# An adaLN block with a test-time-training layer and a mixture of experts: where the updated expert weights live, and how many expert blocks are worked beside the last chunk

## The reference, cut to what matters

```python
h = _layernorm(x) * (1 + ca) + sa
x = x + ga * attn(h)      # 2 sequences of 1024 rows, 4 heads of 128
h = _layernorm(x) * (1 + cb) + sb
x = x + gb * ffn(h)       # 8 experts, the best 2 for each row

# attn: a scan over chunks of 128 rows; state w0, w1, w2 for each head
def step(carry, inp):
    gate = ki @ w0_ ; hb = ki @ w2_ ; hidden = silu(gate) * hb
    dhidden = vi @ w1_.T   # and the gradients from it
    w1g = newtonschulz5(hidden*lr1 , vi) ; w0g = ... ; w2g = ...   # 2 steps, bf16
    w_i = (w_i + w_ig), each column scaled back to its first norm
    oi = silu(qi @ w0_) * (qi @ w2_) @ w1_

# ffn: each expert's weights carry a low-rank addition
gup = xf @ gate_up_proj[e] + 2 * (xf @ A_e.T) @ B_e.T
out = (silu(gates) * up) @ down_proj[e] + 2 * (...)
y   = out[best] * w0 + out[second] * w1       # the two best of softmax(router)
```

## Time and profile before

| | |
|---|---|
| time, three runs | 967.18, 969.18, 971.17 us |
| the profiled execution | 967.96 us |
| its span, first to last instruction | 966.2 us |
| TensorE busy | 863.2 us, 89% |
| VectorE, ScalarE, GpSimdE busy | 68%, 67%, 36% |
| moved by DMA | 120.41 MB |

### The profile page before, as it was taken

How to read it: one execution, slowest core, us unless ns; L and a number is a source line. 1 busy time by engine, 2 the same in 40 slices (tenths; PEclk the granted TensorE clock), 3 DMA queues, 4 the chain that set the end, 5 groups by cost and what they waited for, 6 DMA issues and landing times.

```text
span 966.2 us, 16204 instructions
## 1 busy us (share of the span) xinstructions
PE 863.2 (89%) x5128; PEld 525.3 (54%) x5128; DVE 661.3 (68%) x2312; ACT 647.3 (67%) x1416; POOL 349.4 (36%) x284
## 2 busy tenths in 40 slices
PE   7887999989999899998999989898288899999995
PEld 3545565765657656476564755656153344444442
DVE  3487889898898988989889898896365222222231
ACT  2675888888888888888888888885272333344331
POOL 2221454444544445444454444442033122222222
PEclk8898999999999999999999999998699999999998
DMA  9744353351632516335163250439603445554540
GB/s 332 275 143 150 104 186 94 105 170 40 186 102 97 166 44 186 98 100 165 45 187 90 76 161 32 127 99 357 285 23 66 99 80 90 91 88 82 90 71 0
DMA packets 59091, 120.41 MB, mean 125 GB/s; under 512 B 6897, under 2 KB 8561, under 8 KB 57985
## 3 DMA queue, kind: packets, MB, share of 16 engines
q1 hardware_dynamic: 50688, 102.28, 34.0%
q0 software_dynamic: 8176, 16.85, 9.3%
q10 hardware_dynamic: 144, 0.26, 0.1%
HBM read 51.94 MB, written 69.27 MB: 125 GB/s over the span
## 4 chain that ended last, share of the span: by engine, by line
PE 39%; DVE 10%; DMA 8%; POOL 5%; issue 3%; ACT 2%; SPq 0%; POOLq 0%
PE bank L924 12%; PE bank L943 6%; DMA xs_scratch<-t_arena 5%; PE bank L125 5%; PE bank L119 5%; DMA t_arena<-xs_scratch 2%; POOL xs_scratch L2435 2%; DMA wm_scratch<-t_arena 1%; POOL t_small L2422 1%; PE bank L586 1%; POOL t_small L2401 1%; PE bank L494 1%; PE bank L514 1%; PE bank L595 1%; PE bank L563 1%
## 5 line engine op out<-in xcount | busy, mean ns | idle before, releaser
L119 PEld LDWEIGHTS bank<-t_arena 128*128 128x128 bf16 (+1 forms) x1536 | 123.4, 122 | 82.9 <-issue 15.7
L119 PE MATMUL bank<-t_arena 128*128 128x128 bf16 (+1 forms) x1536 | 152.3, 236 | 6.4 <-DVE t_arena L1073 1.9
L125 PE MATMUL bank<-t_ident,t_arena 128*128 128x128 f32 x618 | 102.7, 286 | 29.2 <-DVE t_arena L1354 8.1
L924 PE MATMUL bank<-t_arena 128*128 x272 | 123.0, 595 | 2.5 <-ACT t_arena L2352 2.5
L125 PEld LDWEIGHTS bank<-t_ident,t_arena 128*128 128x128 f32 x618 | 72.6, 144 | 84.9 <-issue 36.7
L2525 POOL DMA_INDIRECT out_x<-t_arena,t_tokx x34 | 53.0, 1559 | 151.8 <-DVE t_small L1848 141.7
L1851 DVE TENSOR_TENSOR t_arena<-t_arena,bank 128x256 f32<-128x256 f32 x34 | 14.3, 421 | 102.8 <-ACT t_arena L2343 102.8
L2343 ACT ACTIVATE t_arena<-bank 128x256 f32<-128x256 f32 x34 | 13.1, 385 | 105.9 <-PE bank L924 105.9
L924 PEld LDWEIGHTS bank<-t_arena 128*128 128x128 f32 x272 | 48.9, 189 | 51.7 <-issue 51.7
L2416 POOL TENSOR_TENSOR t_small<-t_small,t_half 128x8 f32<-128x8 f32 x15 | 26.0, 1733 | 109.9 <-DVE t_small L1252 109.9
L943 PE MATMUL bank<-t_arena 128*128 x136 | 64.1, 593 | 0.6 <-ACT t_arena L2338 0.6
(11 more groups left out here) (773 smaller groups left out, 2242.4 us busy)
## 6 DMA issues: line engine op xcount, KB each, us to landing
xs_scratch<-t_arena SPq DMA_DIRECT2D x16, 2064.0 KB, 11.7
wm_scratch<-t_arena SPq DMA_DIRECT2D x48, 256.0 KB
t_arena<-wm_scratch SPq DMA_DIRECT2D x8, 1536.0 KB
t_arena<-xs_scratch SPq DMA_DIRECT2D x39, 258.0 KB, 2.7
t_arena<-in_gate_up SPq DMA_DIRECT2D x32, 256.0 KB, 3.4
t_arena<-in_wmod SPq DMA_DIRECT2D x6, 1024.0 KB, 11.0
t_arena<-in_down SPq DMA_DIRECT2D x16, 256.0 KB, 3.7
out_x<-t_arena SPq DMA_DIRECT2D x16, 256.0 KB, 2.0
```

The source lines that it names most:

```text
L119: mm = pe.matmul(bank[:, s], lhs[:, s], rhs[:, s], start=True, stop=True)
L125: mm = pe.transpose(bank[:, 128 * k:128 * k + 128], src[:, 128 * k:128 * k + 128], idn)
L924: mm = pe.matmul(AA(u)[:, :], xT[u % 2][:, 128 * k:128 * k + 128], w_e[:, bass.ds(which[u], 1), 512 * k:512 * k + 512], start=(k == 0), st ...
```

## The change: what it does, and the diff

Experts 1, 3 and 5 are kept. Their 18 tiles are loaded at the place in SBUF where the products will read them, are updated there, and are not stored or read back. The other 30 tiles are staged in the still unused parts of those three places, are stored as before, and only their five experts are read back, in the order 6, 7, 0, 2, 4. The tiles of the chunks have other places too: the projection and low-rank weights now lie where experts 0, 2 and 4 go, and the preparation's tiles where 6 and 7 go. The output's transposed tile `oT` is gone, and `ap_s` takes its role. The two groups of turn 0 are one; each turn c does group c, and the sixteenth group is done in chunk 15 (L719 in the new file). `EB` is 8, so 8 blocks are worked beside chunk 15 and 31 in the loop. The order of the steps in chunk 15 is written anew on all engines.

```diff
+EB = 8
 NF = 2 * NC + NE - 1 - EB
...
+KEPT = (1, 3, 5)
 
 
 def units():
-    left = [[(2 * q + i, k) for i in range(2) for k in range(6)] for q in range(4)]
-    without = (3, 2, 1, 0, 3, 2, 1, 0, 3, 2, 1, 0, 3, 2, 3)
-    out = [[left[q].pop(0) for q in range(4) if q != without[m]] for m in range(NC - 1)]
-    return out + [left[2] + left[3]]
+    left = [[(2 * q, k) for k in range(6)] + [(2 * q + 1, k) for k in (4, 5, 0, 1, 2, 3)] for q in range(3)]
+    left.append([(e, k) for e in (6, 7) for k in range(6)])
+    return [[left[q].pop(0) for q in range(4) if q != (m % 3 if m < 12 else 3)] for m in range(NC)]
 
 
 UNITS = units()
+
+STORED = [sum(e not in KEPT for n in range(m + 1) for e, k in UNITS[n]) for m in range(NC)]
...
+        def place(m, j):
+            e, k = UNITS[m][j]
+            if e in KEPT:
+                return w_e[:, e, 512 * k:512 * k + 512]
+            return w_e[:, KEPT[j], 512 * (m % 4):512 * (m % 4) + 512]
+
+        wqkv = [w_e[:, 2 * j, 0:2048].rearrange("p (k n) -> p k n", k=4) for j in range(3)]
+        la = [w_e[:, 2 * j, 2048:2816] for j in range(2)]
+        lb = cut(14336, 512, 2)
...
+                pe.wait_ge(prep_act, nth(PREP_ACT, min(c + 1, NC - 1), "kT"))
+                pe.wait_ge(prep_act, nth(PREP_ACT, min(c + 1, NC - 1), "vT"))
+                pe.wait_ge(prep_act, nth(PREP_ACT, min(c + 1, NC - 1), "qT"))
                 if c == 0:
-                    pe.wait_ge(prep_act, nth(PREP_ACT, 1, "kT"))
-                    pe.wait_ge(prep_act, nth(PREP_ACT, 1, "vT"))
-                    pe.wait_ge(prep_act, nth(PREP_ACT, 1, "qT"))
-                    for j, (e, k) in enumerate(UNITS[0]):
-                        q = slice(32 * (e // 2), 32 * (e // 2) + 32)
-                        mm = pe.matmul([P0, P1, P2][j][:, :], la[e % 2][q, 128 * k:128 * k + 128], lb[k // 4][q, :], start=True, stop=True)
-                    mm.then_inc(mgf_pe, 1)
-                pe.wait_ge(prep_act, nth(PREP_ACT, c+1, "kT"))
-                pe.wait_ge(prep_act, nth(PREP_ACT, c+1, "vT"))
-                pe.wait_ge(prep_act, nth(PREP_ACT, c+1, "qT"))
-                if c == 0:
-                    pe.wait_ge(mgf_dve, nth(MGF_DVE, 0, "u2"))
+                    pe.wait_ge(mod_dve, nth(MOD_DVE, 0, "lae"))
                 if c >= 1:
                     pe.wait_ge(mg_dve, nth(MG_DVE, c-1, "u2"))
-                for j, (e, k) in enumerate(UNITS[c + 1]):
+                if c == NC - 1:
+                    pe.wait_ge(ta_dve, nth(TA_DVE, 0, "f0"))
+                for j, (e, k) in enumerate(UNITS[c]):
...
+            for j, (e, k) in enumerate(UNITS[15]):
+                q = slice(32 * (e // 2), 32 * (e // 2) + 32)
+                mm = pe.matmul([P0, P1, P2][j][:, :], la[e % 2][q, 128 * k:128 * k + 128], lb[k // 4][q, :], start=True, stop=True)
+            mm.then_inc(mg_pe, 1)
+            pe.wait_ge(n1_dve, nth(N1_DVE, NC - 1, "rs"))
+            pe.matmul(B1[:, 0:4], ones[:, :], nss[1], start=True, stop=True).then_inc(n1_pe, 1)
...
+            pe.wait_ge(s_e, 80)
+            for k in range(4):
+                mm = pe.matmul(AA(0)[:, :], xT[0][:, 128 * k:128 * k + 128],
+                               w_e[:, bass.ds(which[0], 1), 512 * k:512 * k + 512], start=(k == 0), stop=(k == 3))
+            mm.then_inc(up_pe, 1)
...
-                if c == 0:
-                    dve.wait_ge(mgf_pe, nth(MGF_PE, 0, "mg"))
-                    dve.wait_ge(s_st[0],48)
-                    dve.scalar_tensor_tensor(out=stage[0][0], in0=P0[:, :], scalar=2.0, in1=stage[0][0], op0=ALU.mult, op1=ALU.add).then_inc(mgf_dve, 1)
-                    dve.scalar_tensor_tensor(out=stage[0][1], in0=P1[:, :], scalar=2.0, in1=stage[0][1], op0=ALU.mult, op1=ALU.add).then_inc(mgf_dve, 1)
-                    dve.scalar_tensor_tensor(out=stage[0][2], in0=P2[:, :], scalar=2.0, in1=stage[0][2], op0=ALU.mult, op1=ALU.add).then_inc(mgf_dve, 1)
                 dve.wait_ge(mg_pe, nth(MG_PE, c, "mg"))
-                dve.wait_ge(s_st[(c + 1) % 4],48 * ((c + 1) // 4 + 1))
-                dve.scalar_tensor_tensor(out=stage[(c + 1) % 4][1], in0=P1[:, :], scalar=2.0, in1=stage[(c + 1) % 4][1], op0=ALU.mult, op1=ALU.add).then_inc(mg_dve, 1)
...
+                dve.scalar_tensor_tensor(out=place(c, 1), in0=P1[:, :], scalar=2.0, in1=place(c, 1), op0=ALU.mult, op1=ALU.add).then_inc(mg_dve, 1)
...
+            dve.scalar_tensor_tensor(out=place(15, 1), in0=P1[:, :], scalar=2.0, in1=place(15, 1), op0=ALU.mult, op1=ALU.add).then_inc(mg_dve, 1)
...
-                    sp.wait_ge(s_ms, 48 * (m - 3))
+                    sp.wait_ge(s_ms, 16 * STORED[m - 4])
                 for j, (e, k) in enumerate(UNITS[m]):
                     src = A["gate_up"][e][128 * k:128 * k + 128, :] if k < 4 else A["down"][e][128 * k - 512:128 * k - 384, :]
-                    sp.dma_start(stage[m % 4][j], src).then_inc(s_st[m % 4], 16)
+                    sp.dma_start(place(m, j), src).then_inc(s_st[m % 4], 16)
 
             def store_tiles(m):
+                sp.wait_ge(mg_dve, nth(MG_DVE, m, MG_DVE[-1]))
                 for j, (e, k) in enumerate(UNITS[m]):
-                    sp.dma_start(wm_dram[e][:, 512 * k:512 * k + 512], stage[m % 4][j]).then_inc(s_ms, 16)
+                    if e not in KEPT:
+                        sp.dma_start(wm_dram[e][:, 512 * k:512 * k + 512], place(m, j)).then_inc(s_ms, 16)
...
-                if c == 0:
-                    sp.wait_ge(mgf_dve, len(MGF_DVE))
-                    store_tiles(0)
-                    load_tiles(4)
...
-                if c + 2 < NC:
-                    sp.wait_ge(mg_dve, nth(MG_DVE, c, MG_DVE[-1]))
-                    store_tiles(c + 1)
-                if c + 5 < NC:
-                    load_tiles(c + 5)
+                if STORED[c] > (STORED[c - 1] if c else 0):
+                    store_tiles(c)
+                if c + 4 < NC:
+                    load_tiles(c + 4)
 
             sp.wait_ge(prep_pe, len(PREP_PE) * NC)
-            sp.wait_ge(s_ms, 48 * (NC - 1))
-            for n in range(2):
-                sp.wait_ge(s_z[n], 8 * NC)
-            expert(0)
-            expert(1)
-            expert(4)
-            sp.wait_ge(mg_dve, nth(MG_DVE, NC - 2, MG_DVE[-1]))
-            store_tiles(NC - 1)
             sp.wait_ge(rate_pe, len(RATE_PE) * NC)
             sp.wait_ge(prep_act, len(PREP_ACT) * NC)
             sp.wait_ge(prep_dve, len(PREP_DVE) * NC)
-            expert(2)
+            sp.wait_ge(s_ms, 16 * STORED[NC - 1])
+            expert(6)
             sp.wait_ge(fwd_pe, len(FWD_PE) * (NC - 1))
             for sem in (n0_pe, n1_pe, n2_pe):
                 sp.wait_ge(sem, len(N0_PE) * (NC - 1))
-            expert(3)
-            sp.wait_ge(s_ms, 48 * NC)
-            sp.wait_ge(s_o[0], 16 * (NC // 4))
-            for e in range(5, NE):
-                expert(e)
+            expert(7)
+            sp.wait_ge(mg_pe, len(MG_PE) * NC)
+            expert(0)
+            expert(2)
+
+            for n in range(2):
+                sp.wait_ge(s_z[n], 8 * NC)
+            expert(4)
...
+            sp.wait_ge(s_sa, 16)
+            at = sp.value_load(row0u[0:1, 6:6 + 1], min_val=0, max_val=2048 * NE - 128)
+            sp.dma_start(xg[6 % RING], xs[bass.ds(at, 128), :]).then_inc(s_g[6 % RING], 16)
+            sp.wait_ge(s_sa, 32)
+            at = sp.value_load(row0u[0:1, 7:7 + 1], min_val=0, max_val=2048 * NE - 128)
+            sp.dma_start(xg[7 % RING], xs[bass.ds(at, 128), :]).then_inc(s_g[7 % RING], 16)
```

More of the change, by code:

```diff
@@ L18 @@
 NE = 8
-EB = 5
+EB = 8
 NF = 2 * NC + NE - 1 - EB
@@ L585, in _ @@
                 if a >= 0:
-                    pe.matmul(A0[:, :], oT[:, 128:256], wproj[:, 1, :], start=False, stop=False)
+                    pe.matmul(A0[:, :], ap_s[:, 128:256], wproj[:, 1, :], start=False, stop=False)
                 if 0 <= c < NC:
```

943 lines of the change are left out of this document (534 added, 409 removed).

## The result

The changed kernel takes 943.35 us, the median of four runs (938.78 to 945.25), against 968.18 us for the kernel before beside it. The ratio is 0.9734, 95% interval 0.969 to 0.9779. The forecast was 946.5, and 946.0 for the profiled execution, which took 945.25 us (span 943.5). That one is the slowest of the four; five more runs of the same kernel, later, gave a median of 943.46.

The account below looks back on a forecast made before the run. The prediction took the kernel as a row of TensorE work, apart from a stop in chunk 15 and a wait in turn 0. Terms -5.9, 0, -14.2, -1.5, +0.5, -0.9 sum to -22.0: 946.5 us, range 938 to 955.

Parts of the forecast that it names:

- the likeliest case: Whole kernel: the forecast of 946.5 us, own range 941 to 951, chance 0.65.
- my own signs of being wrong: Whole kernel: chunk 15 lasts over 103 us, the turns grow, or TensorE still stops for over 7 us.
- Turn 0: Start: with one low-rank group, TensorE's wait between two groups goes and turn 1 starts at about 83.6; -5.9 us.
- Turns 1 to 14: Turns before chunk 15: same instructions in the same order, only tiles at other places; 0 us.
- The stop: Chunk 15: block 0 lands at 676.7, VectorE arrives about 674.4 and waits 2.3 us in place of 16.5; -14.2 us.
- Clock: Chunk 15 behind TensorE's stop: the work lost at half clock comes back; -1.5 us, bounds 0 and -2.5.
- Group 15: Inside chunk 15: three products where the gradients' norms are waited for, and three VectorE additions; +0.5 us, bounds 0 and +3.
- Three more blocks: Moved from loop into chunk 15: 2.0 us of idle filled, 1.1 lost in stage three; -0.9 us, bounds -6 and +3.
- Rival B: Chunk 15: wait moved but not gone, block 0 at 681.5, TensorE stops 7 us; 952 us (951 to 957), chance 0.10.
- Rival C: Chunk 15: blocks stand in line on their banks; full 975 us, chance 0.03; mild 954 to 960, chance 0.06.
- Rival D: Start: nothing gained, since turn 1 finds another wait where turn 0's was; 952 us, chance 0.03.
- Rival A: Chunk 15: gather lands before VectorE asks and the blocks fill idle time; 939 us (936 to 941), chance 0.13.

Follow-up runs that it names:

- two groups again: Changed kernel with turn 0's group of low-rank products and additions done twice, TensorE waiting for the additions as in the kernel before: 952.16 us.
- both: Changed kernel with group 15 moved early and the gathers of blocks 0 to 3 issued ahead of expert 4: 939.93 us, then 938.04 us.

## Why the prediction was right

The time is inside the likeliest case's own range, and the places where it was won are the ones forecast. That it came within 1 us for the profiled execution (945.25 against 946.0) is luck. Chunk 15 was to grow by 1.4 us (97.9 against 96.46) and grew by 3.8 (100.40 against 96.56); all ahead of it was to gain 5.9 us and gained 8.8; the loop came as forecast. The two misses, 2.4 and 2.9 us, cancel. And one of my own signs of being wrong came true: TensorE still stops for over 7 us, with a stretch at half clock behind the stop. By the steps:

- *Turn 0, -5.9.* Right: -5.5 between the same two marks, and 5.3 back when the wait is put back. Turn 1 began at 83.26, where 83.6 was forecast; that this fits so well is chance, since in like kernels it begins anywhere from 79.90 to 83.71. The difference between the marks is what counts.
- *Turns 1 to 14, 0.* 0.7 us came off the turns and 1.8 off turn 14's end. The second is a half-clock stretch that the kernel before had there and that I had missed. Both profiles with the old program have it (the group takes 1.99 and 2.15 us) and none of those with the changed one, *two groups again* among them (1.13), so turn 0's wait is not its cause. Which part of the change is, no run shows.
- *The stop, -14.2.* This is the step that was mis-sized: -9.2. What is left of the stop, 7.4 us, is just past its bound of 7. The landing of block 0 was nearly right, 675.3 against 676.7 (by its own terms 662.3 + 12.1 + 2.1 = 676.5). What failed is "it arrives at about 674.4": VectorE was at the reader at 668.8. I had moved its whole stage by the 5.9 us of turn 0 and added the work put between. But chunk 15 came 8.8 us earlier, and in the old order VectorE had waited 1.16 us for a norm's product that TensorE issued late, and for half-clock products, neither of which came back. Group 15 was early for the same reason: 658.75, where I had 662.3. Yet the gather did not gain those 3.5 us: from there to the landing are 16.5 us, where I had 14.2. So the landing was right by two misses that nearly cancel. The queue wasn't empty when the three experts were issued (expert 7 landed at about 660.2), and 6.28 MB moved in those 16.5 us, not the 4.98 of my sum; that the rest is in part the gathers of blocks 1 to 5, issued from 664.5 on, is my reading, and no run tested it. I also set VectorE's wait (2.3) against TensorE's stop (16.5), though VectorE's own wait was 17.81. The rate that I took, 0.41 MB/us, was what the queue moved while full (418 to 430 GB/s between 662.6 and 670.6). The 358 GB/s of the Trainium skill (DMA: Bandwidth & Descriptors, "Where 436 GB/s comes from") does not hold for this queue, with one core running.
- *Clock, -1.5.* This did not come. Behind the stop there is still a stretch at half clock; stage two is at 0.91 in place of 0.89, and stage three, which was at 1.00, is at 0.96. What came back is ahead of the stop, 0.89 to 1.00.
- *Group 15, +0.5.* Moving it earlier costs TensorE 0.82 us at the norms in its place, and the group shows no wait where it stands.
- *Three more blocks, -0.9.* Together with the clock and group 15 I had -1.9 for the rest of chunk 15 and the loop; the table has 2.3 + 10.7 - 17.7 = -4.7. The sum was 2.8 us short, and the reason was not mine. I priced a block by the idle time that it fills, and looked for it behind the stop. The wait that matters is the loop's first gather, which I called "covered" in half a sentence. With the new order of blocks 0 to 4 it is covered by block 7 alone, and without the three blocks, in that order, the kernel is 13 us slower.

Rival B had the size of the wait, "moved but not gone", with TensorE stopping for 7 us, but not its reason: it wanted group 15 3 us late and the queue at 0.36, block 0 at 681.5, and group 15 was early and the queue faster. It was cheap because behind the stop there are 70.3 us, where the forecast had 25.7 + 49.0 = 74.7. Rival C, blocks in series, did not happen: the idle behind up and down (0.93 and 0.55) is the same as before, and those 70.3 us are shorter than the sum. Rival D fell with the experiment on turn 0. Rival A's time is what the kernel *both* reaches, with two more edits: 938 to 940, where it was given 936 to 941.

What stays open: which activity ahead of it makes the half-clock stretches come and go. One run bears on it: where group 15 no longer stands between the gradients and the projection, the projection begins at half clock, as it did in the kernel before. But the stretches also come and go with no edit at all. Executions of the changed kernel lie between 938.78 and 945.25, and the start-up and these stretches are what differs between its two profiles. The same product of block 5 in the first and in the second:

```profile
728.50 3.51 PE L918 MATMUL bank<-t_arena 128*128 x4
...
728.78 1.98 PE L918 MATMUL bank<-t_arena 128*128 x4
```

## What to carry to other kernels

A small transfer that an in-order engine waits for belongs ahead of the large ones in its queue, as soon as its own data are ready. On the kernel before that alone gave 13.6 us, where the whole change gave 25, at no change in bytes. When work is moved to fill idle time, ask first which latency it covers: count from the last step of the chain (here routing, scatter, gather) to its consumer, and leave as much work behind that step. And where a small producer holds large transfers back, as group 15 did, try moving it; here that brought block 0 only 2 us earlier, for the gather also had to wait for the gradients and the scatter, and it cost a half-clock stretch.
